# Batch and block loops of a two-stage transformer layer: written-out code against loops on the engines

## The reference

```python
x = _layernorm(x + attn(x))   # q, k split in a plain and a rotary part, 16 query heads, 4 key heads;
                              # keys 0..767 are averaged in 12 groups of 64, the last 256 are kept;
                              # scores masked by position, softmax, times v, times Wo (1024 x 512)
x = _layernorm(x + ffn(x))    # the ffn:
    x = fwht(x * SU_ug) / 64
    x = silu(x @ W_gate.T * s1) * (x @ W_up.T * s0)          # 512 -> 2048
    x = fwht(x * SU_dp) / 64
    x = x @ W_down.T * s2                                    # 2048 -> 512
```

## Time and profile before

| | us |
|---|---|
| median of 3 runs | 1619.06 (1616.49 to 1619.58) |
| the profiled execution, its own time | 1619.06 |
| its span in the profile | 1617.3 |
| attention, four batches and the start | about 0 to 547 |
| feed-forward, eight blocks | about 547 to 1617 |

### The profile page before, as it was taken

One profiled execution on the slowest core, in us unless ns is written; L12 is line 12 of the kernel. 1 busy time (PEld: TensorE's weight loads), 2 busy tenths in 40 slices (PEclk: granted clock), 3 DMA queues, 4 the chain that ended last, 5 costly groups with the idle time before them and its releaser, 6 DMA issues.

```text
span 1617.3 us, 26393 instructions
## 1 busy us (share of the span) xinstructions
PE 1540.3 (95%) x10152; PEld 1380.3 (85%) x10152; DVE 1065.6 (66%) x1835; ACT 617.2 (38%) x1255; POOL 463.6 (29%) x584
## 2 busy tenths in 40 slices
PE   6989989998998689999999999999999999999997
PEld 5977977887886578889999999999999999999996
DVE  6876777677677488885565566466457557557544
ACT  4153244235226344543343343333333333333322
POOL 5365356446337343330030030040030022003001
PEclk9999999999999789999999999999999999999998
DMA  7031022122220587677767767776866867766861
GB/s 265 19 111 48 33 90 87 34 79 98 68 79 27 190 317 260 245 275 252 257 225 258 270 211 253 272 247 221 295 218 239 297 211 249 279 240 214 282 238 49
DMA packets 92059, 307.42 MB, mean 190 GB/s; under 512 B 9888, under 2 KB 10272, under 8 KB 90144
## 3 DMA queue, kind: packets, MB, share of 16 engines
q1 hardware_dynamic: 90928, 301.54, 53.1%
q10 hardware_dynamic: 1008, 4.20, 0.6%
HBM read 255.37 MB, written 50.33 MB: 189 GB/s over the span
## 4 chain that ended last, share of the span: by engine, by line
PE 61%; DVE 4%; issue 1%; ACT 0%; POOL 0%; POOLq 0%; DVEq 0%; ACTq 0%
PE ff_bank_b L1744 16%; PE ff_bank_c L1744 10%; PE ff_bank_a L1744 10%; PE ff_acc L94 7%; PE ff_acc L96 7%; PE ff_acc L95 7%; DVE ff_d_lo L1558 1%; PE ff_x_ps L1715 1%; PE ff_x_ps L1697 1%; DVE ff_ring L1548 0%; PE ff_x_ps L1705 0%; DVE ff_x_lo L1543 0%; PE ff_x_ps L1706 0%; DVE ff_c L1598 0%; DVE ff_c L1604 0%
## 5 line engine op out<-in xcount | busy, mean ns | idle before, releaser
L1744 PE MATMUL ff_bank_b<-ff_x_hi,ff_ring 128*128 128x256 f32 x1536 | 304.8, 281 | 8.6 <-DVE ff_c L1598 5.1
L1744 PEld LDWEIGHTS ff_bank_b<-ff_x_hi,ff_ring 128*128 128x128 f32 x1536 | 249.7, 189 | 10.3 <-DVE ff_ring L1548 7.1
L1744 PE MATMUL ff_bank_b<-ff_x_lo,ff_ring 128*128 128x256 f32 x768 | 215.4, 280 | 0.0
L1744 PE MATMUL ff_bank_a<-ff_x_hi,ff_ring 128*128 128x256 f32 x1024 | 204.8, 283 | 5.0 <-issue 5.0
L94 PE MATMUL ff_acc<-ff_d_hi,ff_h_hi 128*128 128x512 f32 x512 | 204.4, 399 | 2.7 <-DVE ff_d_lo L1558 2.7
L1744 PE MATMUL ff_bank_c<-ff_x_hi,ff_ring 128*128 128x256 f32 x1024 | 205.4, 283 | 0.0
L96 PE MATMUL ff_acc<-ff_d_hi,ff_h_lo 128*128 128x512 f32 x512 | 200.5, 392 | 0.0
L95 PE MATMUL ff_acc<-ff_d_lo,ff_h_hi 128*128 128x512 f32 x512 | 200.1, 391 | 0.0
L1744 PEld LDWEIGHTS ff_bank_a<-ff_x_hi,ff_ring 128*128 128x128 f32 x1024 | 166.4, 189 | 8.1 <-issue 5.4
L1744 PEld LDWEIGHTS ff_bank_c<-ff_x_hi,ff_ring 128*128 128x128 f32 x1024 | 165.9, 189 | 2.2 <-issue 1.7
L1598 DVE TENSOR_TENSOR ff_c<-ff_bank_b,ff_c 128x512 f32<-128x512 f32 x64 | 44.2, 690 | 163.4 <-PE ff_bank_b L1744 163.4
(11 more groups left out here) (303 smaller groups left out, 3417.0 us busy)
## 6 DMA issues: line engine op xcount, KB each, us to landing
ff_ring<-gu_scratch SPq DMA_DIRECT2D x392, 512.0 KB, 5.0
gu_scratch<-ff_ring SPq DMA_DIRECT2D x56, 512.0 KB, 3.8
at_xt<-in_xt SPq DMA_DIRECT2D x4, 2048.0 KB, 8.1
at_xn<-in_x SPq DMA_DIRECT2D x32, 256.0 KB, 3.1
x_scratch<-at_x SPq DMA_DIRECT2D x32, 256.0 KB, 2.0
ff_raw<-in_wgu SPq DMA_DIRECT2D x8, 1024.0 KB, 6.5
at_wd_a<-in_wd SPq DMA_DIRECT2D x8, 512.0 KB, 4.6
mixed_scratch<-at_wd_a SPq DMA_DIRECT2D x8, 512.0 KB, 3.2
```

The costliest lines, as they stand in the source:

```text
L1744: i = pe.matmul(bank[:, m, :], r[:, a, m, c, :], b[:, k, c, :], start=(k < 3 and m == 0 and c == 0 and b is x_hi and a == 0), stop=(m == 1 ...
```

## The change

Ten Python loops become loops that the engine itself runs (`Fori`): one instruction stream for the body, a counter in a register, and a compare and branch at the end. In attention, batches 0, 1 and 2 are three turns of a loop on each of the five engines, and batch 3 is written out behind it. In the feed-forward part block 0 and block 7 are written out, and blocks 1 to 6 are three turns of a loop over pairs of blocks on PE, ACT, DVE and SP. POOL has its own loop of 6 turns there.

```diff
-            for b in range(B - 1):
+            with pe.Fori(0, B - 1) as b:         # likewise on sp, pool, act and dve
                 batch(b, True)
             batch(B - 1, False)
...
-        def blocks(body):
-
-            for blk in range(FBLK):
-                body(blk, blk // 2, blk % 2, blk == 0, blk == FBLK - 1)
+        def blocks(eng, body):
+
+            body(0, 0, 0, True, False)
+            with eng.Fori(0, FBLK // 2 - 1) as pair:
+                body(pair * 2 + 1, pair, 1, False, False)
+                body(pair * 2 + 2, pair + 1, 0, False, False)
+            body(FBLK - 1, FBLK // 2 - 1, 1, False, True)
...
-            blocks(body)
+            blocks(sp, body)                     # likewise act, dve, pe
...
-            for blk in range(FBLK - 2):
+            with pool.Fori(0, FBLK - 2) as blk:
                 inverse_deviation(blk)
                 pair_sums(blk + 2)
                 butterfly(blk + 2)
```

More of the change, by code:

```diff
@@ L326, in tiles @@
                         store_down(1)
-            for b in range(B - 1):
+            with sp.Fori(0, B - 1) as b:
                 tiles(b, True)
@@ L451, in _ @@
             pool.wait_ge(wo_lo_s, 8)
-            for b in range(B - 1):
+            with pool.Fori(0, B - 1) as b:
                 batch(b, True)
@@ L615, in _ @@
                 act.activation(wo_hi[:, c, :], wo_raw[c], ACT.Copy).then_inc(wo_hi_s, 1)
-            for b in range(B - 1):
+            with act.Fori(0, B - 1) as b:
                 batch(b, True)
@@ L871, in _ @@
             rotate_pooled_keys(0)
-            for b in range(B - 1):
+            with dve.Fori(0, B - 1) as b:
                 batch(b, True)
@@ L1140, in _ @@
                 local_keys(0, t)
-            for b in range(B - 1):
+            with pe.Fori(0, B - 1) as b:
                 batch(b, True)
@@ L1527, in _ @@
             act.wait_ge(scaled, 3)
-            blocks(body)
+            blocks(act, body)
             for t in range(FT):
@@ L1672, in _ @@
                     lower_product(2 + k // 2)
-            blocks(body)
+            blocks(dve, body)
             dve.wait_ge(*x1_in[1].now(FBLK // 2 - 1, 16))
@@ L1802, in _ @@
                 pe.matmul(acc[:, k, :], w[:, :], begin_lo[v], start=False, stop=True).then_inc(xh_ps.sem, 1)
-            blocks(body)
+            blocks(pe, body)
 def layer_kernel(nc, io, out):
```

## The result

The changed kernel took 1631.31 us (median of 4 runs, 1627.54 to 1631.96), the kernel before beside it 1618.99 us (1616.49 to 1619.58): ratio 1.0068, 95% interval 1.0056 to 1.0082. It is slower by 12.3 us, where 7.1 us were forecast; the time lies inside the range. A later comparison of the same kernel gave 1.0075 (1.0062 to 1.0088).

A forecast was written before the change was run, and what follows sets the result against it. PE was taken as the bound nearly everywhere, without slack in the feed-forward part. Attention seams 2.9, feed-forward seams 3.2 and register work 1.0 made 7.1 us on 1619.06 us: 1626 us, range 1618 to 1636 us.

The forecast's parts named there:

- Rival A: All seams: branches find their target or fetch within the cover; not slower, 1619 to 1620 us; chance 0.30.
- C: Feed-forward pairs: register work behind the wait of L1598 costs 0.2 us in each of 48 pairs; 1635 us; chance 0.05.
- rival B: Branches back: a long fetch, M of 6.3 us or more; 1635 to 1640 us; chance 0.10.
- my own signs of being wrong: Gaps at the seams as before, PE dry ahead of a block's first product (shorter queue), or all blocks evenly longer.
- M: Price of one taken branch back, with its instruction fetch: 3.5 us in attention, 4.2 us in the feed-forward part.
- An attention seam: Branch between batches 0 to 1 and 1 to 2: M less 2.05 us of cover, 1.45 us each, 2.9 us together.
- ACT's share: Attention seam: ACT's branch has 2.05 us of cover ahead of L1011; delay M - 2.05 us, side by side with PE's.
- A feed-forward seam: Branch between blocks 2 to 3 and 4 to 5: M less DVE's 2.6 us of cover, 1.6 us each, 3.2 together.
- handed over while the products before still ran: Feed-forward seam: PE's 24 `down` products are queued early, giving cover of 5.5 us, so M is covered.
- DVE in attention: Attention seam: DVE's branch at 158.9 us, with 4.5 us of cover ahead of L646, costs nothing.
- The clock: PE's clock could fall in a gap, but gaps under 5 us in attention stand at 0.99; no cost counted.
- Register work: Loop register instructions, exposed mainly in attention: 1 us taken, 4 us as high end.

The follow-up runs named there:

- e5: Changed kernel with every loop announcing where its closing branch leads; 1627.26 us, ratio 1.0057 to the kernel before.
- after: First trace of the changed kernel itself, all loops in place, beside the kernel before; 1631.31 us, ratio 1.0068.
- e2: Changed kernel with loops in the feed-forward part alone, attention's batches written out again; 1622.06 us, ratio 1.0024 to the kernel before.
- e1: Changed kernel with loops in attention alone, feed-forward blocks written out again; 1620.74 us, ratio 1.0018 to the kernel before.
- e7: e4 with the first instruction of DVE's feed-forward loop placed at the start of a fetched block; 1625.80 us, ratio 1.0036.
- e11: e10 with PE's two loops alone announcing their branch's target; 1623.71 us, ratio 1.0041 to the kernel before.
- e4: Changed kernel with all engines but PE in loops, PE written out; 1632.52 us, ratio 1.0095 to the kernel before.
- e8: Kernel before, no loops, with 8 to 66 semaphore increments on PE behind feed-forward blocks 0 to 6; 1640.5 us in one run.
- e9: The changed kernel again, unaltered, for a second trace; 1630.54 us, ratio 1.0075 to the kernel before.
- e12: Changed kernel with all loops announcing their branch's target and DVE's feed-forward blocks written out; 1622.40 us, ratio 1.0027 to the kernel before.
- e10: Changed kernel with 8 more semaphore increments at the start of DVE's feed-forward code; 1622.95 us, ratio 1.0032 to the kernel before.
- e3: Changed kernel with only PE in loops, the other engines written out; 1624.38 us, ratio 1.0033 to the kernel before.

## Why the prediction was right, and what it had wrong

Right: the sign; that PE runs dry at the four taken branches; that the branch's target has to be fetched; PE dry ahead of L973 and late at the second use of bank b; no cost inside a body in the feed-forward part; POOL and SP nothing. Rival A (branches hidden) falls with the four gaps, C (register work in each pair) with 854 products in 120 us. e5 shows that the stall is the fetch, since an announced branch takes 0.2 to 0.4 us, and so do the instruction packets within the branches. Of rival B the long fetch didn't come (in after one packet stands within each of PE's branches, and none is over 5.8 us), but the fall of the clock in a gap did. And one of my own signs of being wrong came true: PE was dry ahead of its first product in a block.

What the prediction concluded from a page was looser than it says. The sizes that it takes from "Runtime: NRT & Kernel Launch" of the Trainium skill, section "Instruction fetch mechanics", are 2048 instructions for PE and 512 for the others (128 and 32 KiB, at 256 instructions for 16 KiB), and bodies of 1388, 317 and 488 instructions are shorter than that, so it does not follow from them that PE in attention and DVE must fetch at each branch. The traces show that they do. They also show that the length of a body alone does not tell: ACT's body in the feed-forward part is fetched in after (2.52 and 2.71 us) and not in e2 (0.26 us).

The size was 12.3 us instead of 7.1. By the steps of the sum:

- **M.** I took 3.5 us in attention and 4.2 us in the feed-forward part for every engine. PE's branches took 3.3 to 3.9 us and 4.5 to 5.8 us. DVE's took 2.8 to 3.1 us in either part, ACT's 2.4 to 2.9 us where it fetched. So M is an engine's own. Of PE's extra 1.1 to 2.5 us in the feed-forward part I had 0.7 us.
- **An attention seam, 1.45 us forecast.** The gaps were 1.30 and 1.20 us, in the second trace 0.97 and 1.03, in e1 0.8 and 0.8. The size holds, by two errors that cancel: the cover of PE is 2.9 us and not 2.2 (the branch is reached 0.15 us after the wait ends, not after 0.8 us), and the register work ahead of L973 adds some 0.4 us to the branch. ACT's share of the step was wrong: it didn't fetch, and PE governs.
- **A feed-forward seam, 1.6 us forecast, DVE deciding.** This is the step that failed. It cost 5.0 and 2.5 us, the second time 5.2 and 5.6. First, "handed over while the products before still ran, which I take": the branch was reached 4.0 us ahead of the end, 16 products with their weight loads behind it, so PE's cover is near the 3.9 us that I had as the low end, against an M of 4.5 to 5.8. PE itself lost 0.7 to 2.1 us. Second, one fetch of DVE against 2.6 us of cover costs 0.6 to 0.7 us (the seams of e7 and e11), less than the 1.6 us of the sum. It fetched twice, 2.9 + 2.9 us and more.
- **DVE in attention, "cover 4.5 us, nothing".** It fetched twice there too (2.0 us at L649). Where PE is late by itself this is hidden; where it is not (e4, e7, e11) PE waits 0.5 to 1.1 us ahead of L1011.
- **The clock.** I set it aside because "gaps under 5 us in attention stand at 0.99". Of the 5.0 us at the seam of blocks 2 and 3, 0.96 came ahead of the first product, 2.5 at the second use of bank b, and 1.6 us in the 6 us behind it, whose granted clock is 0.72; behind the longest gap of e8 it was 2.5 us. In the first trace spells at 178 and 312 us cost 1.6 us each. These two I can't put down to the change: e2, whose attention is written out, has such a spell at 308 us, and e9 has neither.
- **Register work, 1.0 us.** 0.9 us in attention (e12), nothing in the feed-forward part.

By the two traces the 11.3 to 12.6 us (up to 1600 us) are thus 7.5 to 10.8 us at the feed-forward seams and 0.2 to 6.2 us in attention, of which some 2 us are the two gaps and the rest is clock and scatter. That the time still came out inside the range is owed to the width of the range: the feed-forward seams were forecast at 3.2 us together.

## What to carry to other kernels

A loop on an engine costs nothing inside its body and one instruction fetch for each branch back, for each engine whose body is not held: count the turns, and compare the 2.4 to 5.8 us measured here with what that engine has queued when it reaches the branch, which the trace shows. Announcing the branch on PE alone took its gaps away without a new stall, but no time was won that can be measured (e11 1623.71 us, e10 1622.95 us on the same chip), so measure it. Look where the top of every other long loop comes to lie (a second fetch close behind the first is the sign), and look behind the exit as well. A change of some padding can then move a kernel by 0.4% without any of its work having changed, so a small gain or loss of an unrelated edit may be only that.

## What the hardware showed that I had not expected

- **A loop's top near a block's end is fetched for twice.** 2.9 to 3.9 us more on DVE (after, e4, e9), none with the top placed or moved by 8 instructions (e7, e10). A packet stands in the hole, and where the top lies in its block is inferred from these runs, not read. Queues of instructions of the page after:

```profile
q8 instruction: 91, 1.49, 0.4%
q14 instruction: 59, 0.48, 0.1%
```

  The earlier trace rows has 82 packets for q8; e4, where all but PE loop, has 82 again and e3, where PE alone does, has 91, so q8 is PE's. Its packets have 16.4 KB, those of q14, the other engines' together, 8.2 KB. "Runtime: NRT & Kernel Launch" of the Trainium skill, section "Instruction fetch mechanics", says that a branch out of the held window forces a fetch, which the trace bears out with 2.4 to 5.8 us, and that engines are filled in 16 KiB blocks; for the engines other than PE the packets here have half that.
- **PE's sequencer ran 16 products and their weight loads ahead, 4.0 us,** not all 48 instructions behind the last wait. "TensorE: Matmul & The Clock Gate" of the Trainium skill, in its table of engine facts, gives a queue of 64; the lead measured here is about half that, and the measurement decides.
- **A branch's length varies within one kernel,** 4.46 and 5.14 us, or 4.54 and 5.78 us, for the same branch. The packets show where the time goes: in all traces PE's packet starts 0.9 to 1.1 us behind the branch in attention and 2.1 to 3.4 us behind it in the feed-forward part, and from there to the end of the branch it is 2.3 to 2.8 us in both. So what varies is the wait until the packet starts. DMA engines are at 0.7 in the feed-forward part and below 0.1 at the attention seams, which fits a wait for them, but isn't shown to be the cause.
- **An announced branch can cost a stall elsewhere,** 3.1 us on DVE 17 us behind the loop's exit (e5), 2.5 and 2.0 us on ACT 56 us behind it (e5, e12), each with an instruction packet in the hole, while PE, announced likewise, had none (e5, e11, e12).
- **The name in a wait can mislead.** "PE ff_bank_a L1747 <- DVE ff_x_lo L1546: 2.1" stands where PE's own branch ended last; with that branch announced and DVE's code the same (e5) it is gone.
